# Attention and its output projection in one stage: a gated two-layer cross-attention block in fp32 on one core

## What is computed

```
x = x + tanh(g_xattn[0]) * xattn0(layernorm(x), ctx)     # 32 heads of 128, 8 kv heads, q and k RMS-normed
x = x + tanh(g_ffn[0])   * scaled_ffn(layernorm(x))
x = x + tanh(g_xattn[1]) * xattn1(layernorm(x), ctx)     # 16 heads of 96, 4 kv heads
x = x + tanh(g_ffn[1])   * routed_lora(layernorm(x))

def xattn(latents, context):                # b = 8, q_len = 112, context 375 rows
    kv = concat([context, latents], axis=1) # 487 rows
    q, k, v = latents @ Wq, kv @ Wk, kv @ Wv
    probs = softmax(scale * q @ k.T)        # 4 query heads share one kv head
    return (probs @ v) @ Wo                 # the out-projection
```

## Time and profile before

| | |
|---|---|
| median of the runs | 3027.71 us (3 runs, 3023.64 to 3032.41) |
| span of the profiled execution | 3023.0 us |
| PE busy | 2842.8 us, 94% of the span |
| ACT, DVE, POOL busy | 1214.6 us, 1164.5 us, 710.5 us |
| layer 0, first score to last matmul of the out-projection | 1150.66 to 1914.80 |
| layer 1, the same | 2549.76 to 2952.60 |

### The profile page before, as it was taken

How to read it: one execution, slowest core, us unless ns; L and a number is a source line. 1 busy time by engine, 2 the same in 40 slices (tenths; PEclk the granted TensorE clock), 3 DMA queues, 4 the chain that set the end, 5 groups by cost and what they waited for, 6 DMA issues and landing times. The chain is left out here.

```text
span 3023.0 us, 43041 instructions
## 1 busy us (share of the span) xinstructions
PE 2842.8 (94%) x14487; PEld 2421.8 (80%) x14487; DVE 1164.5 (39%) x2034; ACT 1214.6 (40%) x2550; POOL 710.5 (24%) x585
## 2 busy tenths in 40 slices
PE   6999999799999997999998999598998998998997
PEld 5888887688888886888886888477998997887885
DVE  4333330411112116777772332643101112776335
ACT  4333332322222216777772323434322223785223
POOL 1111110300000005666655732120000001553400
PEclk9999999899999998999998999798998999999998
DMA  4233333222221213333336721102241222332312
GB/s 143 77 101 101 100 102 112 100 63 68 67 61 61 62 55 110 106 106 106 107 88 158 179 65 55 66 1 79 82 117 56 92 92 79 81 83 71 87 34 63
DMA packets 331149, 259.89 MB, mean 86 GB/s; under 512 B 190160, under 2 KB 285768, under 8 KB 331056
## 3 DMA queue, kind: packets, MB, share of 16 engines
q1 hardware_dynamic: 331056, 258.63, 29.3%
HBM read 190.66 MB, written 67.91 MB: 86 GB/s over the span
## 5 line engine op out<-in xcount | busy, mean ns | idle before, releaser
L42 PE MATMUL kv_y<-kv_whi,kv_xthi 128*125 128x512 f32 (+1 forms) x1152 | 446.0, 387 | 4.6 <-DVE kv_wlo L295 4.2
L44 PE MATMUL kv_y<-kv_whi,kv_xtlo 128*125 128x512 f32 (+1 forms) x1152 | 434.7, 377 | 0.0
L43 PE MATMUL kv_y<-kv_wlo,kv_xthi 128*125 128x512 f32 (+1 forms) x1152 | 433.9, 377 | 0.0
L42 PE MATMUL q_y<-q_whi,xthi 128*128 128x512 f32 (+1 forms) x1008 | 386.3, 383 | 8.0 <-ACT q_qn L487 4.7
L44 PE MATMUL q_y<-q_whi,xtlo 128*128 128x512 f32 (+1 forms) x1008 | 376.7, 374 | 0.0
L43 PE MATMUL q_y<-q_wlo,xthi 128*128 128x512 f32 (+1 forms) x1008 | 376.2, 373 | 0.0
L1000 DVE TENSOR_TENSOR at_ptlo<-at_tb,at_pthi 125x448 fp32r<-125x448 f32 (+1 forms) x384 | 238.2, 620 | 143.8 <-ACT at_pthi L953 137.9
L42 PE MATMUL o_y<-o_whi,o_ohi 128*128 128x512 f32 (+1 forms) x672 | 267.3, 398 | 14.4 <-DVE o_olo L1163 12.1
L953 ACT ACTIVATE at_pthi<-at_tb 125x448 fp32r<-125x448 f32 (+1 forms) x384 | 210.1, 547 | 136.2 <-PE at_tb L909 131.9
L43 PE MATMUL o_y<-o_wlo,o_ohi 128*128 128x512 f32 (+1 forms) x672 | 263.9, 393 | 0.0
L44 PE MATMUL o_y<-o_whi,o_olo 128*128 128x512 f32 (+1 forms) x672 | 263.8, 393 | 0.0
(11 more groups left out here) (192 smaller groups left out, 4819.9 us busy)
## 6 DMA issues: line engine op xcount, KB each, us to landing
kv_xin<-in_ctx_dram SPq DMA_DIRECT2D x48, 500.0 KB
q_raw<-in_L_xattn_Wq_dram SPq DMA_DIRECT2D x8, 2048.0 KB, 8.5
o_raw<-in_L_xattn_Wo_dram SPq DMA_DIRECT2D x64, 256.0 KB, 2.6
qT_d<-q_stage SPq DMA_DIRECT2D x56, 256.0 KB, 2.6
at_qr<-qT_d SPq DMA_DIRECT2D x64, 224.0 KB, 3.2
o_rb<-rT_d SPq DMA_DIRECT2D x32, 448.0 KB
v_d<-kv_stage SPq DMA_DIRECT2D x48, 250.0 KB
kT_d<-kv_stage SPq DMA_DIRECT2D x48, 250.0 KB, 4.5
```

Of the source, the lines that this page charges most:

```text
L42: pe.matmul(out, stat_hi, mov_hi, start=start, stop=False)
L43: pe.matmul(out, stat_hi, mov_lo, start=False, stop=False)
L44: return pe.matmul(out, stat_lo, mov_hi, start=False, stop=stop)
```

## The change

`attention` and `out_project` become one stage, `attend`, for each layer:

- The units are taken with the batch innermost: 8 units (one for each batch) make a group, all of the same kv head. Once a group is done its 4 heads are known for all tokens, and the out-projection for these 4 heads can run.
- The out-projection of a group is cut in 14 pieces, one for each half of Wo and tile of tokens. A piece is NK products accumulated in one PSUM bank (`y`), and DVE adds it to x at once. NK is 4 in layer 0. In layer 1 the 4 heads of 96 are packed in 3 slices of 128 rows: NK is 3.
- The pieces of group g are worked off in the units of group g + 1: one directly behind T0 (`project_early`, in all but the first unit of a group), one directly behind T2 (`project_late`, in all but the last). The last group's 14 come at the end, over 4 banks. The first group has none.
- The normalisation moves into the unit: the reciprocals are turned by one transpose behind T0 (`turn_sums`), copied by ACT behind H1, written to DRAM by SyncE and read back on all partitions. `take_o` on DVE multiplies the output from PSUM by them. In layer 1 it also moves the fourth head's rows into the three slices, with 4 instructions for 1. ACT then makes the high copy (`cut_o`), POOL the low part.
- The slabs of Wo are cut one in a unit (8 in a group in layer 0, 6 of 8 units in layer 1). In layer 1 PE turns them behind T1, in the bank `y`.
- The scores have 3 PSUM banks for 4. DVE's order becomes M3, `take_o`, L3 at a unit's end. ACT's becomes H2, E2, `cut_o`, H3, E3.
- q, k and v are loaded two to three units ahead. In layer 0, x is loaded right at the start of the stage, 3.7 MB.
- The Fori loops of these stages are gone: the code is written out.

Its core (the three loops over u are those of PE, ACT and DVE, in this order):

```diff
-                ORDER = ["S0", "T0", "S1", "T1", "S2", "S3", "v2", "T2", "v3", "V0", "T3", "V1"]
-                ACT_ORDER = ["T0", "q", "T1", "S0", "S1", "T2", "S2", "S3", "T3", "o"]
-                DVE_ORDER = ["k", "S0", "T0", "S1", "T1", "S2", "S3", "T2", "T3", "o"]
...
+                        def project_piece(q, bank):
+                            g, half, t = piece(q)
+                            i = 2 * g + half
+                            pe.wait_ge(w_lo_s, NK * (i + 1))
+                            pe.wait_ge(o_lo, units_for(g, t))
+                            for k in range(NK):
+                                last = product(pe, bank[:], oh[:, g % 2, k, t * P:(t + 1) * P], ol[:, g % 2, k, t * P:(t + 1) * P],
+                                               w_hi[:, i % 3, k, :], w_lo[:, i % 3, k, :], k == 0, k == NK - 1)
+                            last.then_inc(projected, 1)
...
+                        def project_late(u):
+                            q = late_of(u)
+                            if q is not None:
+                                if q:
+                                    pe.wait_ge(added, q)
+                                if flip:
+                                    pe.wait_ge(w_lo_s, slabs_by(u + 1))
+                                project_piece(q, y)
...
+                        for u in range(U):
+                            more = u + 1 < U
+                            if more:
+                                scores(u + 1, 0)
+                            turn(u, 0)
+                            turn_sums(u)
+                            project_early(u)
+                            if more:
+                                scores(u + 1, 1)
+                            turn(u, 1)
+                            turn_slab(u)
+                            if more:
+                                scores(u + 1, 2)
+                            if u:
+                                multiply(u - 1, 2)
+                            turn(u, 2)
+                            project_late(u)
+                            if more:
+                                scores(u + 1, 3)
+                            if u:
+                                multiply(u - 1, 3)
+                            multiply(u, 0)
+                            turn(u, 3)
+                            multiply(u, 1)
...
+                        for u in range(U):
+                            more = u + 1 < U
+                            high(u, 0)
+                            if u + 2 < U:
+                                cut_q(u + 2)
+                            high(u, 1)
+                            copy_sums(u)
+                            if more:
+                                exp(u + 1, 0)
+                                exp(u + 1, 1)
+                            if u % NB in SLAB_AT:
+                                cut_slab(slabs_by(u))
+                            high(u, 2)
+                            if more:
+                                exp(u + 1, 2)
+                            if u:
+                                cut_o(u - 1)
+                            high(u, 3)
+                            if more:
+                                exp(u + 1, 3)
...
+                        for u in range(U):
+                            more = u + 1 < U
+                            invert(u)
+                            if u + 2 < U:
+                                cut_k(u + 2)
+                            if more:
+                                neg_max(u + 1, 0)
+                            low(u, 0)
+                            if early_of(u) is not None:
+                                add(early_of(u), y)
+                            if more:
+                                neg_max(u + 1, 1)
+                            low(u, 1)
+                            if flip and u % NB in SLAB_AT:
+                                cut_slab(slabs_by(u))
+                            if more:
+                                neg_max(u + 1, 2)
+                            low(u, 2)
+                            if late_of(u) is not None:
+                                add(late_of(u), y)
+                            if more:
+                                neg_max(u + 1, 3)
+                            if u:
+                                take_o(u - 1)
+                            low(u, 3)
```

More of the change, by code:

```diff
@@ L873, in _, with scores @@
+                        cut_o(U - 1)
                     @block.tensor
                     def _(pe):
-                        def scores(p, h, half, u):
+                        def scores(u, h):
+                            m, p = G * u + h, u % 2
                             if h == 0:
[L878 to L883, removed]
@@ L916, in _ @@
[L916 to L922 removed]
+                                pe.wait_ge(q_cut, u + 1)
+                                pe.wait_ge(k_cut, u + 1)
+                            if m >= 3:
+                                pe.wait_ge(exped, m - 2)
@@ new lines, in scores, with turn @@
+                            product(pe, s[m % 3][0:QLEN, 0:KVPAD], qs[:, p, 0, h * QLEN:(h + 1) * QLEN], qs[:, p, 1, h * QLEN:(h + 1) * QLEN],
+                                    ks[:, p, 0, :], ks[:, p, 1, :], True, True).then_inc(scored, 1)
+                        def turn(u, x):
+                            m, p, r = KVT * u + x, u % 2, ROWS[x]
+                            if x == 0:
+                                pe.wait_ge(exped, G * u + G)
+                            if m >= 2:
+                                pe.wait_ge(lo_done, m - 1)
+                            for h in range(G):
+                                last = pe.transpose(tb[x % 2][0:r, h * QLEN:(h + 1) * QLEN], pr[:, p, h, x * CR:x * CR + r], ident[0:QLEN, 0:QLEN])
+                            last.then_inc(turned, 1)
@@ new lines, in add @@
+                        def add(q, bank):
+                            g, half, t = piece(q)
+                            if source is not None and q == 0:
+                                dve.wait_ge(x_loaded, 16 * TT)
+                            dve.wait_ge(projected, q + 1)
+                            cols = x_sb[:, t, half * BANK:(half + 1) * BANK]
+                            dve.scalar_tensor_tensor(out=cols, in0=bank[:], scalar=gate, in1=cols, op0=ALU.mult, op1=ALU.add).then_inc(added, 1)
@@ L1179, in scaled_ffn @@
+                        take_o(U - 1)
+                        first = PIECES * (NG - 1)
+                        for i in range(PIECES):
+                            add(first + i, tail_banks[i % 4])
+                next_stage()
         def scaled_ffn(x_sb):
```

601 lines of the change are left out of this document (279 added, 322 removed).

## The result

The kernel after takes 3083.72 us (median of 4 runs, 3079.33 to 3086.10), the kernel before 3026.11 us beside it: 1.0184 times as long, with an interval of 1.0169 to 1.0199, so 58 us slower. The forecast was 3060 us, 32 above the 3027.7 it started from, with 3042 to 3078 as its own range and 2985 to 3108 as the wide one. Its sign and its mechanism held; its size was a little over half of what came, and the time lies 6 us above its own range.

What follows compares the result with a forecast made beforehand. PE was taken to bound both stages. Layer 0 +24 us, layer 1 +9 and first units -1.5 sum to +32 on 3023.0: span 3055, median 3060 (chance 0.46), own range 3042 to 3078, 8 in 10 2985 to 3108.

Steps and rivals of the forecast that it cites:

- What bounds the kernel: Both stages of each layer before the change: PE never without work inside them, little idle for the weave to fill.
- my list: Savings: layer 1's 168 fewer matmuls 38.1 us, fewer turned slabs 3.6; stage borders 13.3 and 11.5; turn of the half.
- The PE-only sum: Merged stages if PE never waited: layer 0 751.5 against 764.1 us, layer 1 351.5 against 402.8; together -64 us.
- Rival A: Both merged stages: PE never waits, faster by 64 us at most, 2964 us; chance 0.16.
- The chain in layer 0: Unit ends: T0 waits for E3 behind `cut_o`, H3 and `take_o`; 1.3 us lost in first-group units, 0.33 with two pieces; +24 us.
- The chain in layer 1: Unit ends and slabs: two-piece units with a slab take 13.54 us where PE needs 11.35; layer 412.0 us, +9.
- The slab's wait: Layer 1, two-piece units with a slab: the late piece waits for the slab to leave bank `y`; PE loses 1.5 us.
- Rival B: New waits in both layers: the clock falls there, 75 us more at most, 3135, or 3097 with half; chance 0.20.
- Rival C: Layer 0's margins hold and some layer 1 waits are shorter: about 0 change, 3030 us; chance 0.18.
- What I costed at nothing: POOL in the first group (6.9 of 8.2 us), slabs' and sums' transfers, load of x, fetching loop-free code: no cost taken.
- The load of x: Start of layer 0: 3.67 MB in 9.1 us should just fit ahead of k and q; at 175 GB/s costs up to 9.

Runs made afterwards that it cites:

- e8_start: e3_tail_slab with the reciprocal ahead of L3 on DVE, and the second unit's q and k cut in the middle of the first four steps: 2970.7 us.
- e7_take: Kernel after, layer 1 alone, without the three narrow instructions of `take_o` from the third unit on (output partly wrong): 3053.5 us.
- e1_tail: Kernel after with the end of ACT's unit in the order E3, H3, `cut_o` instead of `cut_o`, H3, E3: 3012.8 us.
- e3_tail_slab: e1_tail's edit to the kernel after, plus ACT cutting layer 1's slab right behind H1, before the sums and first two exps: 2986.3 us.
- e6_sums_q: e3_tail_slab with the reciprocal ahead of L3 on DVE, and the second unit's q cut ahead of the first four exps on ACT: 2974.2 us.
- e9_start_late: e8_start with the late piece behind v3 instead of directly behind T2: 2969.2 us.

## Why the prediction was right in sign and short in size

**What bounds the kernel.** Right: PE was the bound in all four stages, and there was little for the weave to fill. With next to no waits the merged L0 (e8_start, 761.6 us) is 2.6 us shorter than the two stages of before; L1 (355.1) is 47.8 shorter, of which my list gives 38.1 to the 168 matmuls and 3.6 to the slabs.

**The PE-only sum.** Near: 751.5 and 351.5 us forecast, 761.6 and 355.1 reached by e8_start. Two-piece units take 12.43 for 12.33 us, 4 us in 42 units, and the first group another 5. Rival A's 2964 us was a fair figure for a weave without waits, and the best kernels came to 2969. It was not this kernel's case.

**The chain in layer 0.** Right, hop by hop. Forecast 8.24, 12.66, 9.94 and 10.94 us; measured 8.33, 12.80, 10.05 and 11.09. The wait in a two-piece unit is 12.80 - 12.43 = 0.37 us, forecast 0.33. The hundredths add up: 42 x 0.14 = 5.9 us, 7 x (0.11 + 0.15) = 1.8, the first group 0.4. The start was 1.4 late, by the wait for POOL's q: T0 at 1155.02, 10.0 us after the first score for 8.6. The last unit and the 14 last pieces took 47.5 us for 46.7. Together that is the 10 us.

**The chain in layer 1.** The place was right, and here the size failed, 433.3 for 412.0 us. Two terms of the sum were mis-sized. The first is the chain's length. The sum has "`take_o` is 4 instructions, by the same row about 1.15 us": it took 1.36. The late piece started 7.25 us after T0 for 7.1. With these and the other hops two-piece units with a slab were 13.98 for 13.54 us (15 x 0.44 = 6.6 us), the others behind the first group add 4, the start 1.6, the end 1.4. The second is the clock in the first group, which the sum had at full speed: that group took 81.1 us for 73.7, and 6.3 of it is the clock, by e7_take. The sum had the clock's fall as a rival only, not as a term. The slab's wait was 1.17 us, forecast 1.5.

**Rival B (the clock falls).** In part. Apart from the stage starts it fell in the first group of layer 1 alone. L0 kept 0.99 with a wait in each of its units, and the rest of layer 1 kept 0.99 with a wait at T0 and another for the slab in most of them. So some 6 us came of the 75.

**Rival C.** Wrong: no margin of layer 0 held. One wait of layer 1, the slab's, was shorter than forecast, but all its units behind the first group were longer.

**What I costed at nothing.** POOL was no bound: the first group of e8_start has units of 6.9 us. The load of x just fitted: in the kernel after DVE waits for k's load at the two stage starts alone.

```profile
DVE at_k L1174 <- DMA at_kr<-kl_d: 42.6, 2, 21.5
```

The fetch of the code that is written out cost nothing that shows. Window of e8_start, L0 from its second group to its last unit: PE has work in flight all the time.

```profile
1214.18:1861.12 646.94, 646.94 (x3418) 553.54 (x3416) 394.04 (x702) 345.98 (x880) 379.71 (x329) 1.00 0.37 104
```

## What to carry to other kernels

When two stages are woven, list for each queue what stands ahead of the instruction that the bounding engine waits for, and ask of each whether it is needed for it. Here two copies that nobody needed soon stood ahead of the exponential that all needed: the kernel was 2% slower than before, and with the exponential first it is 0.5% faster (e1_tail), with the slab's copy earlier too 1.3% (e3_tail_slab). Costs of a loop show in its period, not in the list of waits: 94 late units were 46 waits there. A queue's order is cheap to try; a dose of one dummy instruction, at two places of the same queue, tells load from place.

## What the runs showed of the hardware

DVE's cast of k (128x488, SBUF to SBUF) took 0.40 us when POOL was idle. When it began 0.1 us or more behind the start of a POOL subtraction, it ended 0.27 us after POOL's end, however long that made it (in POOL's last 0.1 us it took its own 0.40). Timeline of e3_tail_slab:

```profile
1252.43 1.14 POOL L946 TENSOR_TENSOR at_ol<-at_rb,at_oh 128x448 fp32r<-128x448 f32 x1
...
1252.54 1.30 DVE L1176 CAST at_k<-at_kr 128x488 fp32r<-128x488 f32 x1
```

1252.54 + 1.30 = 1253.84 against 1252.43 + 1.14 = 1253.57. In the kernel after the same cast began later in POOL's instruction and took 0.94 us. In e6_sums_q, e8_start and e9_start_late many casts began 0.02 to 0.04 us behind POOL by the records, and in all of these POOL was the one held. Timeline of e8_start, in a unit with two pieces:

```profile
1248.25 1.46 POOL L946 TENSOR_TENSOR at_ol<-at_rb,at_oh 128x448 fp32r<-128x448 f32 x1
...
1248.28 0.40 DVE L1177 CAST at_k<-at_kr 128x488 fp32r<-128x488 f32 x1
```

The cast kept its 0.40 us, and POOL took 1.46 for 1.15. The Trainium skill, SBUF — State Buffer, section "SBUF: two separate sides", says that GpSimd and DVE share a pair of ports as an exclusive lock, on DVE's side for instructions in a 2-port mode or with two SBUF inputs: whichever starts first has it for the whole instruction, and the other is blocked. The rows agree that one of the two is held until the other is done. In the near-ties the one held is POOL, whose record begins first; no run shows when the lock is taken, nor in which mode the cast ran. So an edit that moves an ACT copy can lengthen a DVE instruction: in L0 from the second group on this cast had a mean of 0.91 us in after, 1.30 in e3_tail_slab and 0.40 in e8_start.

A narrow DVE instruction is not cheap by its size: 32x112 took 0.27 us each, three of them 0.84, while the 96x336 one beside them, 9 times the elements, took 0.50.
